# Last edge pass of a two-layer graph network: projection in three passes, y one turn later, messages scanned from PSUM, the one-hot on ScalarE

## The reference

```python
qkv = x @ W_qkv.T + b_qkv
att = einsum('mhd,mhd->mh', Q[receivers], K[senders]) / sqrt(32)
attention = softmax of att over the edges of one receiver
out0 = segment_sum(attention[:, :, None] * V[senders], receivers) @ W_ff.T + b_ff
x = layernorm(x + out0)
W = (edge_feats @ W_dist + b_dist) * cut[:, None]
msgs = embed_table[node_z][senders] * W
out1 = concat([x, segment_sum(msgs, receivers)], axis=1) @ W_comb + b_comb
x = layernorm(x + out1)
```

## Time and profile before

| | |
|---|---|
| median of 3 runs | 1139.29 us |
| profiled execution, its own time | 1139.81 us |
| its span, first to last instruction | 1138.1 us |
| busy in the span: PE, DVE, ACT, POOL | 93%, 82%, 70%, 71% |
| first and last start of a `num` scan | 760.0 and 1105.9 us |
| granted TensorE clock, mean | 0.976 |

### The profile page before, as it was taken

One profiled execution on the slowest core, in us unless ns is written; L12 is line 12 of the kernel. 1 busy time (PEld: TensorE's weight loads), 2 busy tenths in 40 slices (PEclk: granted clock), 3 DMA queues, 4 the chain that ended last, 5 costly groups with the idle time before them and its releaser, 6 DMA issues.

```text
span 1138.1 us, 25638 instructions
## 1 busy us (share of the span) xinstructions
PE 1062.5 (93%) x7302; PEld 985.0 (87%) x7302; DVE 928.7 (82%) x2662; ACT 794.4 (70%) x2432; POOL 806.9 (71%) x648
## 2 busy tenths in 40 slices
PE   4859999999999999999998799989999999999992
PEld 3759999999999999999877687879998888888882
DVE  4977888888877888777898989768888888888882
ACT  2957777777777777777776778865666666666663
POOL 4367888888888888888796768834666666666663
PEclk9979999999999999999999999989999999999997
DMA  4856666666766566666455557765666666666640
GB/s 150 281 210 216 221 229 218 225 226 217 221 220 221 200 223 223 222 212 211 183 202 189 181 208 238 268 203 165 171 179 182 183 185 184 188 190 190 192 130 33
DMA packets 121387, 227.26 MB, mean 200 GB/s; under 512 B 33587, under 2 KB 61486, under 8 KB 121184
## 3 DMA queue, kind: packets, MB, share of 16 engines
q1 hardware_dynamic: 104000, 189.54, 50.5%
q0 software_dynamic: 17248, 36.08, 10.6%
HBM read 137.84 MB, written 93.59 MB: 203 GB/s over the span
## 4 chain that ended last, share of the span: by engine, by line
PE 47%; DVE 24%; issue 11%; POOL 8%; ACT 6%; DMA 2%; DVEq 1%; ACTq 0%; SPq 0%; POOLq 0%
PE ps L845 9%; PE ps L824 5%; DVE num L1602 5%; PE ps L838 3%; PE ps L882 3%; PE ps L883 3%; PE ps L884 3%; PE ps L839 3%; PE ps L840 3%; DVE zeT L1613 3%; POOL zin L704 3%; DVE agg L1626 3%; DVE est L1639 3%; DVE msg L1622 2%; ACT t L1178 2%
## 5 line engine op out<-in xcount | busy, mean ns | idle before, releaser
L704 POOL TENSOR_TENSOR zin<-xin,bff_row 128x1024 f32<-128x1024 f32 x98 | 235.6, 2406 | 15.8 <-DVE stat L1392 10.2
L1420 DVE SCALAR_TENSOR_TENSOR yn<-ps,r,bc 128x256 f32<-128x256 f32 x391 | 169.2, 474 | 67.2 <-PE ps L840 44.3
L845 PE MATMUL ps<-w_mix,zT 128*128 128x256 f32 x780 | 189.7, 394 | 12.2 <-ACT zT L1081 9.7
L845 PEld LDWEIGHTS ps<-w_mix,zT 128*128 128x128 f32 x780 | 147.3, 196 | 36.5 <-ACT zT L1081 12.6
L1096 ACT ACTIVATE junk<-yn 128x256 f32<-128x256 f32 x391 | 157.7, 415 | 12.9 <-DVE yn L1420 12.9
L1392 DVE BATCH_NORM_STATS2 stat<-zin 128x6 f32<-128x256 f32 x391 | 135.7, 409 | 13.5 <-POOL zin L704 13.5
L733 POOL TENSOR_TENSOR ev<-abc,v 128x512 f32<-128x512 f32 x49 | 62.1, 1268 | 116.0 <-DVE zeT L1613 113.8
L723 POOL DMA_INDIRECT xd<-in_x_dram,idx x98 | 94.5, 964 | 37.4 <-issue 21.8
L745 POOL DMA_INDIRECT out_dram<-oe,idx x98 | 101.7, 1037 | 25.5 <-issue 20.7
L838 PE MATMUL ps<-mix_hi,z_hi 128*128 128x256 f32 x392 | 114.8, 293 | 2.7 <-DVE z_lo L1457 2.7
L726 POOL DMA_INDIRECT xs<-in_x_dram,idx x98 | 93.7, 956 | 29.9 <-issue 28.3
(11 more groups left out here) (210 smaller groups left out, 3390.8 us busy)
## 6 DMA issues: line engine op xcount, KB each, us to landing
xin<-in_x_dram SPq DMA_DIRECT2D x97, 512.0 KB, 4.3
out_dram<-on SPq DMA_DIRECT2D x97, 512.0 KB
xd_o<-xdT SPq DMA_DIRECT2D x49, 256.0 KB
v_o<-vT SPq DMA_DIRECT2D x49, 256.0 KB
v<-v_o SPq DMA_DIRECT2D x49, 256.0 KB
xd<-xd_o SPq DMA_DIRECT2D x49, 256.0 KB, 4.1
abc<-a_o SPq DMA_DIRECT2D x196, 64.0 KB
sbc<-same_o SPq DMA_DIRECT2D x49, 128.0 KB, 3.8
```

The costliest lines, as they stand in the source:

```text
L704: pool.tensor_tensor(z, xx, bb, ALU.add).then_inc(n_z, 1)
L845: last = mm(ps[0:np_, half(g, j), (j % 2) * D:(j % 2 + 1) * D], zT[:, g % 2, k, j * P:j * P + np_], w_mix[:, k, :], start=k == 0, stop=k = ...
L1420: last = dve.scalar_tensor_tensor(out=yn[0:np_, q, j * D:(j + 1) * D], in0=ps[0:np_, half(g, j), (j % 2) * D:(j % 2 + 1) * D], scalar=r1[0 ...
```

## The change

All of it concerns the last edge pass. The projection `ff` goes from fp32 to three passes over high and low parts, as mix has them; the weight is split once early on, and for each block ACT makes the high part of num (`sum_high`) and POOL the low part (`sum_low`). y and what follows it (squares, output, scatter) come one turn later. The product of filter and embedding is written back to its own PSUM bank, from which the scans read it; the next filter product then waits for the scans. The one-hot moves from DVE to ACT, as 1 - (type - lane)^2 below zero cut off: a Square (`off`) and a Relu (`hot`).

```diff
@@ GpSimd
+        def sum_low(n):
+            pool.wait_ge(e_num, 2 * (n + 1))
+            pool.wait_ge(e_nh, n + 1)
+            after(pool, e_ffp, n)
+            pool.tensor_tensor(flat(num_lo), flat(num[:, n % 2]), flat(num_hi), ALU.subtract).then_inc(e_nl, 1)
...
-        for i in range(-1, B + 4):
+        for i in range(-1, B + 5):
...
-            if within(i - 4):
-                scatter(i - 4)
+            if within(i - 5):
+                scatter(i - 5)
+            if within(i):
+                sum_low(i)
             if within(i + 1):
                 weigh(i + 1)
             if within(i - 1):
@@ TensorE
-            pe.wait_ge(e_num, 2 * (n + 1))
+            pe.wait_ge(e_nh, n + 1)
+            pe.wait_ge(e_nl, n + 1)
...
-                    last = mm(bank(FF[par])[:, c, :], wff[:, k, c * P:(c + 1) * P], num[:, par, k, :], start=k == 0, stop=k == DC - 1)
+                    hi, lo = (w[:, k, c * P:(c + 1) * P] for w in (wff_hi, wff_lo))
+                    mm(to, hi, num_hi[:, k, :], start=k == 0, stop=False)
+                    mm(to, hi, num_lo[:, k, :], start=False, stop=False)
+                    last = mm(to, lo, num_hi[:, k, :], start=False, stop=k == DC - 1)
...
             pe.wait_ge(e_atT, n + 1)
-            after(pe, e_msg, n)
+            after(pe, e_agg, 2 * n)
@@ ScalarE
+        def onehot(n):
+            par = n % 2
+            act.wait_ge(e_tb[par], 16 * (n // 2 + 1))
+            act.activation(off[0:SPECIES, :], tybc[0:SPECIES, par, :], ACT.Square, bias=lane[0:SPECIES, 0:1]).then_inc(e_off, 1)
+            act.wait_ge(e_off, n + 1)
+            after(act, e_embp, n)
+            act.activation(hot[0:SPECIES, :], off[0:SPECIES, :], ACT.Relu, bias=one_col[0:SPECIES, :], scale=-1.0).then_inc(e_hot, 1)
...
+        def sum_high(n):
+            act.wait_ge(e_num, 2 * (n + 1))
+            after(act, e_ffp, n)
+            act.activation(flat(num_hi), flat(num[:, n % 2]), ACT.Copy).then_inc(e_nh, 1)
...
+            if within(i):
+                sum_high(i)
+            if within(i - 4):
+                edge_final(i - 4)
             if within(i - 3):
-                edge_final(i - 3)
+                edge_squares(i - 3)
...
             if within(i + 1):
                 embedding_copy(i + 1)
-            if within(i - 2):
-                edge_squares(i - 2)
+            if within(i + 2):
+                onehot(i + 2)
@@ VectorE
-            dve.tensor_tensor(msg[:], bank(7), emb[:], ALU.mult).then_inc(e_msg, 1)
+            dve.tensor_tensor(bank(7), bank(7), emb[:], ALU.mult).then_inc(e_msg, 1)
...
-                dve.tensor_tensor_scan(out=agg[:, now, c, :], data0=sbc[:, par, :], data1=msg[:, c, :],
+                dve.tensor_tensor_scan(out=agg[:, now, c, :], data0=sbc[:, par, :], data1=bank(7)[:, c, :],
...
             if within(i):
                 sums(i)
                 messages(i)
+            if within(i - 4):
+                edge_rstd2(i - 4)
             if within(i - 3):
-                edge_rstd2(i - 3)
+                edge_y(i - 3)
             if within(i - 1):
                 edge_z(i - 1)
-            if within(i + 2):
-                onehot(i + 2)
             if within(i - 2):
                 edge_stats(i - 2)
-                edge_y(i - 2)
```

More of the change, by code:

```diff
@@ L123, in build @@
     z_lo = sb("z_lo", [P, 2, DC, ROWS * P], F32R)
-    wff = sb("wff", [P, DC, D])
+    wff_hi, wff_lo = (sb(n, [P, DC, D], F32R) for n in ("wff_hi", "wff_lo"))
     wd = sb("wd", [RBF + 1, D])
@@ L217, in build @@
     hot = lp("hot", [P, EB], F32R)
-    emb, msg = (lp(n, [P, 2, EB]) for n in ("emb", "msg"))
+    off = lp("off", [P, EB])
+    emb = lp("emb", [P, 2, EB])
     ev, num, zeT = (lp(n, [P, 2, 2, EB]) for n in ("ev", "num", "zeT"))
@@ L231, in build @@
     ze_hi, ze_lo = (z_lo[:, 0, c, :].rearrange("p (c n) -> p c n", c=2) for c in range(DC))
+    num_hi, num_lo = (z_lo[:, 1, c, :].rearrange("p (c n) -> p c n", c=2) for c in range(DC))
     xdT, vT = (sb(n, [P, 2, 2, EB]) for n in ("xdT", "vT"))
@@ L357, in build @@
     e_hot = sem("onehot_ready")
+    e_off = sem("squared_type_distances")
     e_embp = sem("embedding_product")
@@ L365, in build @@
     e_zp = sem("edge_z_transposed")
+    e_nh = sem("attention_sum_high_parts")
+    e_nl = sem("attention_sum_low_parts")
     e_zh = sem("edge_z_high_parts")
@@ L857, in weight_transposes @@
             after(pe, s_wtc, 3 * k)
-            after(pe, s_wlo, 2 * k)
+            after(pe, s_wlo, 3 * k)
             for r in range(4 * DC):
@@ L942, in ff @@
             par = n % 2
-            pe.wait_ge(e_num, 2 * (n + 1))
+            pe.wait_ge(e_nh, n + 1)
+            pe.wait_ge(e_nl, n + 1)
             after(pe, e_z, 2 * (n - 1))
             for c in range(2):
+                to = bank(FF[par])[:, c, :]
                 for k in range(DC):
-                    last = mm(bank(FF[par])[:, c, :], wff[:, k, c * P:(c + 1) * P], num[:, par, k, :], start=k == 0, stop=k == DC - 1)
+                    hi, lo = (w[:, k, c * P:(c + 1) * P] for w in (wff_hi, wff_lo))
+                    mm(to, hi, num_hi[:, k, :], start=k == 0, stop=False)
+                    mm(to, hi, num_lo[:, k, :], start=False, stop=False)
+                    last = mm(to, lo, num_hi[:, k, :], start=False, stop=k == DC - 1)
             last.then_inc(e_ffp, 1)
@@ L1031, in _ @@
                 pe.wait_ge(s_wtc, 6)
-                pe.wait_ge(s_wlo, 4)
+                pe.wait_ge(s_wlo, 6)
                 pe.wait_ge(s_brow, 2)
@@ L1121, in weight_copies @@
             act.activation(w_hi[:, k, 2 * D:3 * D], ps[:, A + 1, 0:D], ACT.Copy).then_inc(s_wtc, 1)
-            act.activation(wff[:, k, :], ps[:, A + 1, D:2 * D], ACT.Copy).then_inc(s_wtc, 1)
+            act.activation(wff_hi[:, k, :], ps[:, A + 1, D:2 * D], ACT.Copy).then_inc(s_wtc, 1)
         def parts(n):
@@ L1244, in _ @@
         scaled(0)
-        for i in range(-1, B + 3):
+        onehot(0)
+        for i in range(-1, B + 4):
             if within(i + 1):
@@ L1384, in edge_indices @@
             dve.wait_ge(s_lane, 1)
-            dve.tensor_copy(lane[:], lane_i[:]).then_inc(s_idx, 1)
+            dve.tensor_scalar(lane[:], lane_i[:], -1.0, None, ALU.mult).then_inc(s_idx, 1)
         def stats(g):
@@ L1478, in weight_low @@
             dve.tensor_tensor(w_lo[:, k, 2 * D:3 * D], ps[:, A + 1, 0:D], w_hi[:, k, 2 * D:3 * D], ALU.subtract).then_inc(s_wlo, 1)
+            dve.tensor_tensor(wff_lo[:, k, :], ps[:, A + 1, D:2 * D], wff_hi[:, k, :], ALU.subtract).then_inc(s_wlo, 1)
         def bias_parts():
@@ L1599, in sums @@
             after(dve, e_num, 2 * n)
-            after(dve, e_ffp, n - 1)
+            after(dve, e_nh, n - 1)
+            after(dve, e_nl, n - 1)
             for c in range(2):
@@ L1620, in messages @@
             dve.wait_ge(e_emb, n + 1)
-            after(dve, e_agg, 2 * n)
-            dve.tensor_tensor(msg[:], bank(7), emb[:], ALU.mult).then_inc(e_msg, 1)
+            dve.tensor_tensor(bank(7), bank(7), emb[:], ALU.mult).then_inc(e_msg, 1)
             dve.wait_ge(e_msg, n + 1)
@@ L1715, in _ @@
         dve.wait_ge(c_same, 16 * NCH)
-        for i in range(-2, B + 3):
+        for i in range(B + 4):
             if within(i):
```

## The result

The changed kernel took 1192.74 us (median of four runs, 1191.26 to 1196.87) against 1139.41 of the kernel before in the same session: a ratio of 1.0475, 95% interval 1.0454 to 1.0495. It is slower by 53 us; the forecast was 39 slower, with 1196 as the upper end of the range. The profiled execution has a span of 1191.1.

What follows compares the result with a forecast made beforehand. The chain of waits on DVE, with PE only a little behind, bound the 7.26 turn. 7.92 + 0.15 = 8.07 a turn gave +37.3 over 46 turns, +1.7 at the end: 1178.8, or 1178 against the median; range 1157 to 1196.

Steps and rivals of the forecast that it cites:

- the queue's loop: SP's ordered loads, last edge pass: sbc comes late behind the one-hot; 16.05 over two turns, 7.92 each with PSUM scans.
- rival 1: Only the port bites, the loads come early enough: 7.75 a turn, 1164 us; chance 0.17.
- the port's collision: POOL's z_low falling between num's two DVE scans, both reading SBUF: one of three collisions, 7.78 a turn.
- rival 3: Nothing gets late, PE's 6.95 and DVE's 6.88 decide: 6.95 a turn, 1127 us; chance 0.08.
- rival 2: Queue and port both bite in full, z_low blocking num each turn: 0.5 in place of 0.15, 1195 us; chance 0.11.
- What goes: Work and waits the change removes: 0.31 a turn on PE's projection; on DVE the one-hot and both waits before y.
- DVE's own loop: DVE's turn if nothing else is late: num to zeT 5.20, plus 1.43 and 0.25, making 6.88.
- PE's turn: PE's time per turn with the three-pass projection: 7.26 less 0.31, at most 6.95.
- The PSUM scans: Aggregate scans reading messages from PSUM: priced at 0 to -0.12 each, taken as -0.1 a turn.
- SP's run from tybc to sbc: SP's issue time between these two loads: 3.42 before, less 0.38 for v's wait for ev, so 3.04.
- The port: num on DVE and POOL's SBUF reads exclude one another: 0.15 a turn added to the queue's loop, bounds 0 and 0.5.
- What would have shown it wrong: sbc landing well before num, num at 0.74 beside a running z_low, or a turn under 7.26.

Runs made afterwards that it cites:

- three edits that each break it: Changed kernel with sbc first in SP's turn (1165.91 us), with the one-hot back on DVE (1167.20), or with the one-hot earlier in ACT's order (1166.05).

## Why the prediction was right, and where its size was off

The forecast (slower, 1178, range 1157 to 1196) named the mechanism and was 15 us short; the range held with 3 us to spare. Its rivals turned out to be the floors below, one under another: 8.38 a turn with the queue's loop, 7.76 without it (rival 1: 7.75), 6.87 without the port's collision (rival 3: 6.95). The measured 1192.74 lies at rival 2's 1195, but not for its reason: one of num's two scans is over 0.9 in 20 of 49 turns, not in each.

- **What goes.** DVE's own loop was priced at 6.88; it measured 6.87 as soon as nothing else was late. PE's turn, priced at 6.95 at most, is 6.87. Three passes give 0.23 a turn (7.10 to 6.87) once PE decides, not 0.31.
- **The one-hot.** Of its 0.35 on DVE 0.26 were put on the chain. Once z_low is late that is wrong: it fits beside ev. With it on DVE the turn is 6.87 in the median and 6.94 on average, with it on ACT and sbc first 6.87 and 6.90. Taking it off DVE was worth at most 0.05, and the two times (1128.52 and 1125.95) have ratios whose intervals overlap.
- **The PSUM scans.** Priced at -0.1 a turn by the long scans of the earlier trace rows. At 256 elements there is nothing, as the medians before and after show (ns, min/median/max):

```profile
L1626 DVE TENSOR_TENSOR_SCAN agg<-sbc,agg,msg x96: 724/739/753, 765.3 to 1107.9; 128x256 f32<-128x256 f32 x96
```

```profile
L1663 DVE TENSOR_TENSOR_SCAN agg<-sbc,agg,ps x96: 720/734/748, 768.0 to 1158.9; 128x256 f32<-128x256 f32 x96
```

What the place is worth is the port: 89 us, where z_low stands beside them.
- **The queue.** Right, by three edits that each break it. The terms of the loop, over two turns (forecast; median and mean, from the starts and ends of the instructions, over the 39 turns whose num starts between 800 and 1130):

| step | forecast | median | mean |
|---|---|---|---|
| emb's end to hot's end | 0.92 | 0.94 | 0.94 |
| to tybc; tybc to sbc | 0.03 + 3.04 | 0.02 + 3.30 | 0.03 + 3.52 |
| landing of sbc | 3.80 | 3.78 | 3.87 |
| landing to num | 0.25 | 0.02 | 0.04 |
| num to the end of y, PSUM scans and port included | 4.43 - 0.20 + 0.30 | 4.48 | 4.68 |
| y to mix | 0.17 | 0.06 | 0.11 |
| mix to z_high | 1.62 | 1.78 | 1.83 |
| z_high; std1, t2, emb | 0.61 + 1.18 | 0.63 + 1.16 | 0.63 + 1.16 |

The means sum to 16.81, so 8.40 a turn; the forecast had 16.15. **The term that was mis-sized is SP's run from tybc to sbc**, with 0.48 of the 0.66. 3.04 came from one turn with the whole wait of v for ev, 0.38, taken off. But v takes 0.47 where it doesn't wait (904.67 in the timeline above) and 0.32 behind its wait, so the median only fell from 3.43 to 3.30. Single turns run up to 5.8, with 2.9 of that in one issue of abc, and the mean, 3.54 before, is still 3.52; the runs don't tell why an issue is long.

From num to the end of y, turns in which POOL left num alone take 4.43, as forecast; the PSUM scans gave none of their 0.20, and the port added 0.25 in place of 0.30. The 0.25 put between the landing and num came out at 0.04.

The step at mix is 0.21 longer than forecast. 0.16 of that is in the median turn: its twelve matmuls span 1.40 from the first start to the last in place of 1.30, and z_high follows 0.10 behind them in place of 0.04. The rest is the clock. In two stretches the granted clock fell, here beside one that kept it and with one piece of the first by itself:

```profile
878.00:895.00 17.00, 14.93 (x104) 13.79 (x104) 13.04 (x31) 13.09 (x38) 12.81 (x11) 1.00 0.55 162
980.00:1005.00 25.00, 20.54 (x121) 18.74 (x120) 18.45 (x46) 16.58 (x48) 15.90 (x14) 0.86 0.53 160
1002.00:1004.00 2.00, 2.00 (x10) 1.91 (x9) 0.65 (x4) 0.42 (x2) 0.98 (x1) 0.50 0.76 177
1025.00:1036.00 11.00, 8.55 (x49) 7.82 (x49) 9.71 (x26) 8.23 (x26) 7.49 (x7) 0.84 0.49 150
```

At its lowest it is 0.50, the 1.2 GHz level. It fell twice in the first stretch and once in the second, each time after PE had idled before mix, but the length of the pause alone doesn't tell: behind the last of these pauses, longer than the second, it stayed at 1.00 (PE's idle time in brackets):

```profile
983.44 0.38 PE L993 MATMUL ps<-mix_hi,z_lo 128*128 128x256 f32 x1 [2.58 <-DVE ye L1687]
...
1000.81 0.38 PE L993 MATMUL ps<-mix_hi,z_lo 128*128 128x256 f32 x1 [1.88 <-DVE ye L1687]
...
1027.51 0.39 PE L993 MATMUL ps<-mix_hi,z_lo 128*128 128x256 f32 x1 [2.44 <-DVE ye L1687]
...
1128.20 0.39 PE L993 MATMUL ps<-mix_hi,z_lo 128*128 128x256 f32 x1 [2.20 <-DVE ye L1687]
```

In the three slow turns the twelve mix matmuls take 2.03, 2.28 and 1.80 from first to last start in place of 1.40, 1.9 us in all. A pause that the change makes costs PE a second time there; I had no term for it, and it is a small part of the 53 us.

- **The port.** Its bounds, 0 to 0.5 a turn on top of the loop, held, and its stand-alone price of 7.78 was met within 0.03. The collision in the changed kernel, timeline:

```profile
861.11 1.30 POOL L744 TENSOR_TENSOR z_lo<-zeT,z_lo 128x512 fp32r<-128x512 f32 x1 [0.36 <-ACT z_lo L1199]
...
861.65 1.94 DVE L1640 TENSOR_TENSOR_SCAN num<-sbc,num,ev 128x256 f32<-128x256 f32 x2 [1.40 <-DMA sbc<-same_o]
```

num starts 0.54 into z_low and takes 1.94 in place of 1.39: it stands until z_low is over. The rule of the Trainium skill, page "SBUF — State Buffer", section "Who interferes with whom", that the prediction weighed is borne out from both sides: two SBUF operands exclude a POOL operation that reads SBUF (1.72 for a scan beside z_low), one operand does not (1.38 for two scans beside z_low).

- **What would have shown it wrong** did not occur, with one exception: sbc landed 0.02 before num in the median turn, not well before, and no scan of num in the changed kernel kept its 0.75 with more than 0.20 us of it beside a z_low. But six single turns between 787 and 1148 are under 7.26 (down to 6.75), each beside a long one. The loop spans two turns, and no two in a row average below 7.9.

## What to carry to other kernels

Before an instruction is moved later, list what waits in line behind everything that waits for it: here one in-order DMA queue put a load needed at once behind a load needed two turns on, and putting the urgent load first gave back 27 us with no work changed. Floors lie under one another, so the time of removing one obstacle is the next floor, not the full gain: price each alone, since fixing the port without the queue made things worse and fixing both made the change a gain. A wait that is taken off can have been what kept two operations apart on a shared resource; look at what then stands side by side.

## What the hardware showed that I had not expected

- The place of one scan operand (PSUM or SBUF) changed the kernel by 89 us while the scan's own time, with nothing beside it, differs by 0.005.
- A single abc issue on SP took 1.43 where its neighbours took 0.43 to 0.44, with no wait shown in the chain; the runs don't tell why.
- The granted clock fell behind PE's pauses of 2.58, 1.88 and 2.44 us in this pass, and stayed at 1.00 behind one of 2.20 at 1128.
